# A fused adaLN block on one core: V weights split in slot 4, output products in one bank, the second batch normalised beside the first, and a last unit in an order of its own

## The reference

```python
mod = (_silu(L0_c) @ L0_wmod).reshape(L0_c.shape[0], 6, 1, -1)
sa, ca, ga, sb, cb, gb = (mod[:, 0], mod[:, 1], mod[:, 2], mod[:, 3], mod[:, 4], mod[:, 5])
ga = (2 * (ga >= 0) - 1) * jnp.maximum(jnp.abs(ga), 0.25)
gb = (2 * (gb >= 0) - 1) * jnp.maximum(jnp.abs(gb), 0.25)
h = _layernorm(x, axis=-1) * (1 + ca) + sa
x = x + ga * _L0_attn_ref(h, L0_attn_wq, L0_attn_wk, L0_attn_wv, L0_attn_wo)   # rotary, causal softmax
h = _layernorm(x, axis=-1) * (1 + cb) + sb
x = x + gb * _L0_ffn_ref(h, L0_ffn_w12, L0_ffn_b12, L0_ffn_w3, L0_ffn_b3)      # silu(x1) * x2, then @ w3.T
```

## Time and profile before

| | |
|---|---|
| median of three executions | 899.64 us |
| profiled execution, its own time | 897.77 us |
| its span | 896.0 us |
| mean granted clock of PE | 0.951 of 2.4 GHz |
| PE busy | 820.5 us, 92% |
| DVE, POOL, ACT busy | 572.6, 547.6, 504.1 us |
| DMA, mean | 137 GB/s, 122.47 MB |

### The profile page before, as it was taken

The page is one execution under the profiler, slowest core; times in us unless marked ns, Lnnn a source line. Parts: engine busy times, 40 slices in busy tenths (PEclk is TensorE's granted clock), DMA queues, the critical chain, the costliest instruction groups (busy, mean ns, idle before and its releaser), DMA issues.

```text
span 896.0 us, 11652 instructions
## 1 busy us (share of the span) xinstructions
PE 820.5 (92%) x3788; PEld 675.5 (75%) x3788; DVE 572.6 (64%) x1215; ACT 504.1 (56%) x1194; POOL 547.6 (61%) x380
## 2 busy tenths in 40 slices
PE   8889798899999999999999999999999996778897
PEld 2688686687788778877887788778877885557786
DVE  4844656676566657665666666666665674557886
ACT  3232765376657656765676567656765666634410
POOL 1522694568666956695679567946694654492642
PEclk9967999899999999999999999999999998999999
DMA  9403634366355635554555455545544358550011
GB/s 324 160 1 96 175 106 118 101 175 183 86 160 168 175 99 162 161 167 111 161 153 165 117 154 155 163 130 142 163 154 130 106 156 283 152 160 0 1 48 47
DMA packets 104348, 122.47 MB, mean 137 GB/s; under 512 B 7904, under 2 KB 81760, under 8 KB 102240
## 3 DMA queue, kind: packets, MB, share of 16 engines
q1 hardware_dynamic: 103872, 121.67, 46.7%
q10 hardware_dynamic: 416, 0.07, 0.0%
HBM read 77.67 MB, written 44.04 MB: 136 GB/s over the span
## 4 chain that ended last, share of the span: by engine, by line
PE 54%; POOL 16%; ACT 13%; DVE 12%; DMA 2%; issue 2%; SPq 0%; DVEq 0%; ACTq 0%; POOLq 0%
PE q_bank L383 10%; PE o_bank L440 8%; PE x_bank L383 8%; PE out_bank L453 7%; POOL pT_lo L1178 7%; PE s_bank L383 6%; ACT probs L985 4%; PE x_bank L453 4%; POOL wo_lo_sb L1178 4%; ACT probs L993 4%; POOL rope_tmp L1200 2%; PE o_bank L391 2%; ACT pT_hi L962 2%; PE s_bank L634 1%; DVE rope_tmp L676 1%
## 5 line engine op out<-in xcount | busy, mean ns | idle before, releaser
L1178 POOL TENSOR_TENSOR pT_lo<-pT_raw,pT_hi 128x1024 fp32r<-128x1024 f32 (+1 forms) x96 | 193.6, 2031 | 72.7 <-ACT pT_hi L962 72.6
L985 ACT ACTIVATE probs<-probs,neg_max 128x32 f32<-128x32 f32 (+15 forms) x256 | 130.5, 511 | 157.6 <-DVE neg_max L700 157.6
L1178 POOL TENSOR_TENSOR qT<-rope_tmp,qT 128x512 fp32r<-128x512 f32 x64 | 83.3, 1302 | 155.5 <-ACT qT L962 155.5
L700 DVE CUSTOM_DVE_ANT_0 probs<-s_bank,mask_sb 128x32 f32<-128x32 f32 (+15 forms) x256 | 99.3, 436 | 43.7 <-PE s_bank L383 43.4
L1200 POOL TENSOR_TENSOR rope_tmp<-rope_tmp 128x512 f32<-128x512 f32 x80 | 102.7, 1293 | 36.4 <-DVE rope_tmp L677 36.4
L717 DVE STREAM_TRANSPOSE turned<-probs 128x512 f32<-128x512 f32 (+1 forms) x64 | 96.8, 1512 | 42.9 <-DMA spread_dram<-turned 27.8
L383 PE MATMUL s_bank<-kT,qT 128*128 128x32 f32 (+15 forms) x768 | 122.5, 308 | 1.3 <-POOL qT L1178 1.3
L383 PEld LDWEIGHTS s_bank<-kT,qT 128*128 128x128 f32 x768 | 113.0, 189 | 9.1 <-POOL qT L1178 1.7
L993 ACT ACTIVATE probs<-probs,row_inv 128x32 f32<-128x32 f32 (+15 forms) x256 | 111.9, 508 | 0.0
L383 PE MATMUL q_bank<-hT_hi,wq_hi_sb 128*128 128x512 f32 x248 | 101.1, 408 | 5.3 <-DVE rope_tmp L677 5.3
L383 PE MATMUL q_bank<-hT_lo,wq_hi_sb 128*128 128x512 f32 x248 | 99.7, 402 | 0.0
(11 more groups left out here) (247 smaller groups left out, 1805.7 us busy)
## 6 DMA issues: line engine op xcount, KB each, us to landing
spread_dram<-turned SPq DMA_DIRECT2D x64, 256.0 KB, 3.8
pT_raw<-spread_dram SPq DMA_DIRECT2D x16, 1024.0 KB, 5.9
spread_dram<-turned SPq DMA_DIRECT2D x64, 192.0 KB, 3.2
pT_raw<-spread_dram SPq DMA_DIRECT2D x16, 768.0 KB, 5.0
wq_raw<-in_L_attn_wq_dram SPq DMA_DIRECT2D x32, 256.0 KB, 4.9
wo_raw<-in_L_attn_wo_dram SPq DMA_DIRECT2D x8, 1024.0 KB, 5.5
spread_dram<-turned SPq DMA_DIRECT2D x64, 128.0 KB, 5.2
pT_raw<-spread_dram SPq DMA_DIRECT2D x16, 512.0 KB, 4.1
```

The source lines that it names most:

```text
L700: nc.vector.tensor_tensor_reduce(prob_rows(s, t), s_banks[t][:, 0:n].rearrange("p (j s) -> p j s", s=W32), mask_sb[:, T - n:T].rearrange(" ...
L985: nc.scalar.activation(rows, rows, ACT.Exp, bias=neg_max[:, par, t:t + 1], scale=-1.0, accum_out=row_sum[:, par, t:t + 1]).then_inc(exp_do ...
L1178: nc.gpsimd.tensor_tensor(dst, src, hi.bitcast(f32), ALU.subtract).then_inc(done, 1)
```

## The change

The order of each engine's list changes; what is computed does not.

- *Slots.* `wo_high`/`wo_low` move from the end of slot 3 into slot 4, `wv_high`/`wv_low` from slot 5 to the end of slot 4. All output products go to out_bank and wait for the sum of the slot before. The K and V projections wait for `v_lo` or the rotation of K, no longer for a sum. In slot 3 the query projection stands ahead of the output product.
- *Head.* x of batch 1 is loaded ahead of the K weights. Its statistics stand ahead of the first read of the modulation, its normalising between the first rotations. Block 2 is done as columns too; block 3 stands ahead of the third query, block 4 in slot 1 of group 0, blocks 5 and 2 in slot 2.
- *Tail.* Each engine has a `last_unit` written out. DVE makes both parts of the first eight turned blocks (`f_both`); blocks 8 to 11 are turned between the up-products; the last attention and output product stand between up-products 0 and 2; `turn_x1(1)` stands behind up-product 3.

The diff, cut to its core, first PE in the slots:

```diff
-            def project_out(g, s, x_free=None):
+            def project_out(g, s, dst=None):
                 need(pe, attn_lo, SLOTS, g, s + 1)
-                need(pe, wo_added, SLOTS, g, s - 1)
-                dst = x_bank if s % 2 else out_bank
+                dst = dst or out_bank
+                need(pe, wo_added, SLOTS, g, s)
...
+                    if first and s == 1:
+                        modulation(4)
+                    if first and s == 2:
+                        modulation(5)
+                        modulation(2)
+                    if not (last and s == 3):
+                        slot_query(g, s)
                     if s == 3 and not first:
-                        need(pe, v_lo, 2, g, 2)
                         project_out(g, s - 4)
...
                         need(pe, wk_lo, 1, g, 1 + s // TT)
-                        need(pe, wo_added, SLOTS, g, s - 4)
+                        need(pe, v_lo, 2, g, 1 + s // TT)
                         project_k((s // TT + 1) % B, h_lo[1] if first and s == 0 else None)
...
                         need(pe, wv_lo, 1, g, 1 + s // TT)
-                        need(pe, wo_added, SLOTS, g, s - 4)
+                        need(pe, roped, ROPE_GROUP, g, ROPE_FIRST + rope_k_at(s - 2) + 1)
                         project_v((s // TT + 1) % B)
```

POOL in the slots (ACT the same with the high parts):

```diff
+                    if s == 4:
+                        for n in range(REP):
+                            wo_low(g, n)
                     if not (first and s < 2):
                         probs_low(g, s - 2)
...
-                    if s == 3:
-                        for n in range(REP):
-                            wo_low(g, n)
-                    if s == 5 and not last:
+                    if s == 4 and not last:
                         wv_low(g, 1)
```

DVE in the head:

```diff
             norm_x(0)
+            dve.wait_ge(x_in[2], 16)
+            for w in range(TT, 2 * TT):
+                nc.vector.bn_stats(stats[:, w, :], acc[:, w, :]).then_inc(stats_made, 1)
             dve.wait_ge(mod_made, 2)
...
             first_rotation(0)
+            norm_scale(1, 2)
             first_rotation(1)
+            norm_x(1)
             first_rotation(2)
```

PE in the last unit and the tail, and the new function of DVE:

```diff
+            def last_unit():
...
+                project_out(g, 0)
+                pe.wait_ge(v_lo, 2 * KV)
+                project_out(g, 1, dst=x_bank)
+                attend(g, 2)
+                pe.wait_ge(gate_copied, 2)
+                turn_f(0)
+
+                scores(g, 5)
+                project_out(g, 2)
+                turn_f(1)
+                attend(g, 3)
+                pe.wait_ge(f_lo, 2)
+                turn_gate(2)
+
+                scores(g, 6)
+                project_out(g, 3)
...
+            pe.wait_ge(f_lo, 8)
             turn_x1(0)
+            project_out(end, SLOTS - 2)
...
+            up(0, 0)
+            attend(end, SLOTS - 1)
+            up(0, 1)
+            project_out(end, SLOTS - 1, dst=o_bank)
+            turn_f(8)
+            turn_f(9)
+            up(0, 2)
+            turn_f(10)
+            turn_f(11)
+            up(0, 3)
+            pe.wait_ge(wo_added, SLOTS * KV)
+            pe.wait_ge(f_lo, 3 * KC)
+            turn_x1(1)
             up(1, 0)
...
+            def f_both(u):
+                dve.wait_ge(f_turned, u + 1)
+                nc.vector.tensor_copy(f_place(u)[0], f_banks[u][:, :]).then_inc(f_hi_dve, 1)
+                f_low(u)
```

More of the change, by code:

```diff
@@ L384, in product, with modulation @@
                 return last
-            def modulation(m, part):
+            def modulation(m):
                 pe.wait_ge(wmod_in[m], 16)
-                for n in range(part * KC // 2, (part + 1) * KC // 2):
+                for n in range(KC):
                     at = 2 * (KC * m + n)
@@ L574, in _ @@
             project_q(out_bank[:, :], 0, 1)
+            pe.wait_ge(mod_ready, 1)
+            modulation(3)
             pe.wait_ge(roped, 2)
@@ L584, in _ @@
             turn_v()
-            pe.wait_ge(x_normed, B * TT)
-            turn_x(1, range(KC))
-            for m in range(3, 6):
-                modulation(m, 0)
-                modulation(m, 1)
             pe.wait_ge(roped, 4)
@@ L949, in _ @@
             gate_up(0)
-            x1_stats(2 * TT - 1)
+            add_out(end, SLOTS - 1, src=o_bank)
+            for n in range(TT, 2 * TT):
+                x1_stats(n)
+            f_low(8)
+            f_low(9)
             norm_scale(1, B + 2)
-            for u in range(1, TT + 1):
+            gate_up(1)
+            f_low(10)
+            f_low(11)
+            for u in range(2, TT + 1):
                 gate_up(u)
@@ L1108, in _ @@
-            v_high(0, 0, 1)
-            for k in range(KC):
-                modulate_x(1, k)
-            rotated_high(0, 4, qT[0][0][:, :, 3, :])
-            act.wait_ge(b_in, 16)
-            nc.scalar.activation(neg_b1[:, :], b12T[:, 0:KC], ACT.Copy, scale=-1.0)
-            group(0, first=True)
-            for g in range(1, KV - 1):
-                group(g)
-            group(KV - 1, last=True)
-            end = KV - 1
-            f_high(4)
-            probs_high(end, SLOTS - 2)
-            attn_high(end, SLOTS - 3)
@@ L1124, in _ @@
-            probs_high(end, SLOTS - 1)
-            attn_high(end, SLOTS - 2)
-            for u in range(5, 8):
-                f_high(u)
             def norm_x1(b):
@@ L1137, in norm_x1, with group @@
                                          scale=rstd[:, w, :]).then_inc(x1_normed, 1)
+            def group(g, first=False, last=False):
+                for s in range(TT if last else SLOTS):
+                    r = s % TT
+                    exponents(g, s)
+                    q_high(g, s - 1)
+                    if r == 1:
+                        k_high(g, s - 1)
+                    if s == 4:
+                        for n in range(REP):
+                            wo_high(g, n)
+                    normalise(g, s)
+                    if first and s == 3:
+                        act.wait_ge(mod_made, 6)
+                    if not (first and s < 2):
+                        probs_high(g, s - 2)
+                    if r == 2:
+                        v_copy(g, 2 + s // TT)
+                    if not (first and s < 3):
+                        attn_high(g, s - 3)
+                    if r == 2:
+                        v_high(g, (s // TT + 1) % B, 2 + s // TT)
+                    if 1 <= s <= REP and not last:
+                        wq_high(g, s - 1, 1)
+                    if s == 2 and not last:
+                        wk_high(g, 1)
+                    if s == 4 and not last:
+                        wv_high(g, 1)
@@ L1139, in modulate_x1 @@
+            rotated_high(0, 3, qT[0][0][:, :, 2, :])
+            v_copy(0, 1)
+            rotated_high(0, 4, qT[0][0][:, :, 3, :])
+            v_high(0, 0, 1)
+            act.wait_ge(b_in, 16)
+            nc.scalar.activation(neg_b1[:, :], b12T[:, 0:KC], ACT.Copy, scale=-1.0)
+            group(0, first=True)
+            for g in range(1, KV - 1):
+                group(g)
+            group(KV - 1, last=True)
             def modulate_x1(b):
```

433 lines of the change are left out of this document (220 added, 213 removed).

## The result

The change makes the kernel faster by less than forecast: median 875.24 us of four runs (874.39 to 876.92) against 899.77 of the kernel before beside them, a ratio of 0.974 [0.970, 0.977]. The profiled execution took 875.97 us, with a span of 874.2. That is 21.8 us less (24.5 in the medians) where 41 were forecast.

What follows compares the result with a forecast made beforehand. PE was taken as the bound: 54% of the span in the chain of waits, 92% busy, with idle and slow-clock stretches to regain. Terms −12 −7 −22 + 0 = −41 against 897.77 gave 857 us, range 847 to 873.

Steps and rivals of the forecast that it cites:

- Last unit and tail: Last unit and tail: new order, same PE work, DVE sets the pace; 0 us, bounded by −8 and +6.
- The rival with the tail as a gain: Tail: copies and statistics fit DVE's gaps, so the 13 us head start keeps 8 to 10; 848 us, chance 0.18.
- When scores 7 start, both orders stand at about 774: Last unit: old and new order reach scores 7 at about 774, the new with 3.5 us more done.
- The first feed-forward product starts 13 us earlier: Tail: first feed-forward product starts 13 us earlier, with 6.4 us of PE work interleaved into it.
- so step 2 ends at about 836, against 840: Tail, DVE's second gating step: ends at about 836, against 840, with statistics, splits and last sum between the first two.
- Head and group 0, −12: Head and group 0: less idle and half-level time; −8 at the head, −4 in the rest of group 0.
- Second group's first slot, −7: Second group's first slot: the 3.71 us x_bank wait and 3.4 us lost to half clock are regained; −7 us.
- Groups, −3.7 each: Groups 1 to 6: 3.4 us less in slot 6 and 0.3 in slot 4 of each; −22 us together.
- Cost: nothing: Output products' own bank: slot 3's query ahead of the product covers the wait for the sum by 1.5 us; no cost.
- POOL as the bound: Slots 4 to 6: POOL overdraws the spare 0.3 us, each group gains 1.5, not 3.7; 870 us, chance 0.17.
- the clock that doesn't come back: Seven groups: short new waits for wo_lo and vT keep the 1.7 us half-level loss; 869 us, chance 0.10.
- The slower case: Output products: one bank makes PE wait for each sum, 1.0 us for each of 56 gives 913; chance 0.03.

Runs made afterwards that it cites:

- e1: The changed kernel's head and slots with the last group's slots 3 to 7 and the tail as before the change; 857.66 us, 0.953 of the kernel before.
- e5: The changed kernel with gating steps 0 and 1 as early as their inputs on DVE, their exponentials likewise on ACT; 864.09 us, 0.962 of the kernel before.
- e6: The changed kernel with the edits of e3, e4 and e5 together; 858.93 us, 0.957 of the kernel before.
- e11: e6 with the copies of turned weight blocks 4 to 7 back on ACT, DVE making only their low parts; 855.85 us, 0.953 of the kernel before.
- e3: The changed kernel with two output products of the last group's slots 3 and 4 in x_bank, not waiting for the sum just ahead; 869.69 us, 0.966 of before.
- e4: The changed kernel with feed-forward weight and x loads issued behind the block writes of the last group's slot 3; 870.37 us, 0.968 of the kernel before.
- e8: The kernel before with only the V weights' two halves moved from the end of slot 5 to slot 4's; 881.54 us, 0.981 of the kernel before.

## Why the prediction was wrong

The step that failed is **"Last unit and tail"**: forecast 0, bounded by −8 and +6; measured +19.5 in the profile and, by e1 against the change, 17.6 in the medians. The places that lost it, by experiment, are the order of DVE and ACT around the gating (e5, about 10 us by the ratio), the bank whose cover was missing and the loads ahead of the block writes (together e6 against e5, about 5), and the copies on DVE (e11 against e6, about 3). The rival with the tail as a gain had the wrong sign. The other terms sum to −41.3 where I had −41, and e1 gives the forecast time itself; that it agrees so well is partly luck, since the head came 3.2 us short and the groups gave 3.7 more. In the tail, point by point:

- *"When scores 7 start, both orders stand at about 774"*: they came 47.4 us after slot 3 began, against 42.65. I had written that without the query PE would wait 1.3 us for the sum, and did not see that the last group's slot 3 has no query: 1.35 us, and the loads queue 1.6 us later for it. The wait behind the block writes was forecast at 3.9 and was 4.54. e3 prices the place at 5.5 us in the medians, e4 at 4.9, and e6 shows that they overlap.
- *"The first feed-forward product starts 13 us earlier"*: behind scores 7 it does so by 8.3, in all by 3.6. The waits between the two were sized about right, 10.3 us forecast and 11.1 of idle time measured (36.10 − 25.00). What is missing is the clock, 0.81 there: it stands at 0.50 behind the 4.02 us wait and again behind one of 1.61, for 8.4 us of busy time, which loses about 4.2 (an estimate, half of it).

```profile
746.50:751.60 5.10, 5.01 (x12) 3.84 (x12) 3.96 (x19) 2.67 (x8) 2.28 (x1) 0.50 0.17 59
755.20:758.60 3.40, 3.39 (x8) 2.74 (x9) 1.25 (x2) 1.17 (x2) 0.80 (x1) 0.50 0.92 221
```

- *"so step 2 ends at about 836, against 840"* (step 1 in the count from 0): against slot 3 it ends 12.0 us later than before, not 4 earlier. I counted the work between the steps and not what each waits for: step 0 behind a low half that waits for the last attention product, step 1 behind a statistic that waits for POOL. Moving both ahead (e5) gives 1.2%.
- *The clock.* I gave it no term in the tail, though the earlier trace rows had 0.94 there and the earlier trace rows showed 3.4 us at half level behind a 2.07 us wait. It is 10.8 of the 19.5 us. It is no cause of its own: the stretches at half level follow the waits, those of 4.54, 4.02, 1.61 and 7.30 us among them.

Ahead of the tail:

- *Head and group 0, −12:* −8.8. First scores at 55.8, forecast 54.5 (in the other profiled executions with the new head 55.8 to 58.9, with group 1 at 148.3 to 151.0); slot 2 with the double block took 22.0 us at a clock of 0.68, 2 more than my walk. The twelve small operations took 5.2 us, not 6.9: the first three, beside POOL, 0.95 to 1.22, and the others 0.16. By the lock of which the Trainium skill tells ("SBUF — State Buffer", the section on two separate sides) the three would be long and the rest short, and the trace agrees.

```profile
31.26 1.20 DVE L846 TENSOR_TENSOR newton<-rstd 128x4 f32<-128x4 f32 x1
32.50 0.16 DVE L847 SCALAR_TENSOR_TENSOR newton<-newton,var_eps 128x4 f32<-128x4 f32 x1
```

- *Second group's first slot, −7:* 19.07 to 12.28 us, −6.8. Right.
- *Groups, −3.7 each:* −4.3. Slot 4 took 13.39 us, as forecast (13.36); slot 6 12.07, since vT was not 0.6 late. The mechanism holds, but e8 adds to it: 2.7 of the 4.3 are the V split, and 1.6 come with the other edits, of which the bank of its own is the likely one for slot 6. "Cost: nothing" was right in sign for a cost and missed the gain, since the wait for `wv_lo` covered another.
- *Rivals.* POOL as the bound and the clock that doesn't come back are out: 84.40 us at 1.00. By the page "TensorE: Matmul & The Clock Gate" of the Trainium skill (psum-queue depth-cycling) small repeated idle times would swing the clock; two waits of 0.26 to 0.28 us, 1.2 us apart, in every group, did not (clock 1.00). That the head gives nothing is out at −8.8. The slower case is out: only in the last group, where the query was missing, did PE wait for a sum.

## What to carry to other kernels

When an order is written anew, write down for each in-order engine what each instruction waits for and what ready work stands behind it; counting the work between two steps is not enough. A statement such as "the cover is this query" must be looked up at every place where the pattern occurs, first and last rounds above all. A stretch with many waits has to be given a clock term: compare busy time at the same count of matmuls.

## What the runs showed of the hardware

- The same waits (1.38, 1.15 and about 1.15 us) stood ahead of and in up-product 0 in e3, e5, e6 and e11. In e5 and e11 it ran at full level. In e3 and e6 the clock fell at the third wait; in e6 it stood at 0.50 for some 6 us, and the product took 11.43 us and not 8.59. What follows waits of this size is not the same in every execution.

```profile
773.60:776.90 3.30, 3.30 (x8) 2.62 (x9) 0.55 (x1) 1.54 (x3) 2.53 (x2) 0.50 0.00 0
```

- A block of 32 matmul rows of 128x2 takes 3.6 us at full level (from 67.7 in the changed kernel). With PE busy all the time the clock was down soon after: 0.60 over the 11.4 us of the double block, its last 3.4 at 0.50.

```profile
77.00:88.40 11.40, 11.40 (x67) 11.40 (x65) 4.36 (x12) 4.39 (x14) 5.04 (x4) 0.60 0.55 131
```
